# A twelve-layer perceiver in one kernel: an expert layer computed in turned form, and five more value units projected ahead of time

## What is computed

```
L2x:  q = xn @ Wq.T + bq;  k = ctx @ Wk.T + bk;  v = ctx @ Wv.T + bv      # 16 heads of 16
      out = softmax(q k.T / 4, masked) @ v;      x += out @ Wo.T + bo
L0a:  causal linear attention over the 128 rows, gated by a sigmoid;  x += ... @ W_proj
L0f:  y_e = (silu(xn @ W1_e.T) * (xn @ W2_e.T)) @ W3_e.T,  8 experts, 704 wide
      x += sum over the two best experts of score_e * y_e
L2f:  y_e = gelu(xn @ w_up_e.T) @ w_down_e.T,  8 experts, 1024 wide
      out = sum_e weight_e * y_e   (weight_e is zero but for the best two)
      x += layernorm(out) + xn
```

## Time and profile before

| | |
|---|---|
| median of 3 runs | 1596.67 us (1592.42 to 1596.86) |
| profiled execution | 1588.98 us |
| its span, first to last instruction | 1587.2 us |
| mean granted clock of TensorE | 0.992 |
| TensorE busy (matmul, weight load) | 1508.6 us, 1107.0 us |
| VectorE, ScalarE busy | 973.9 us, 954.2 us |

### The profile page before, as it was taken

One profiled execution on the slowest core, in us unless ns is written; L12 is line 12 of the kernel. 1 busy time (PEld: TensorE's weight loads), 2 busy tenths in 40 slices (PEclk: granted clock), 3 DMA queues, 4 the chain that ended last, 5 costly groups with the idle time before them and its releaser, 6 DMA issues.

```text
span 1587.2 us, 33990 instructions
## 1 busy us (share of the span) xinstructions
PE 1508.6 (95%) x13838; PEld 1107.0 (70%) x13838; DVE 973.9 (61%) x1860; ACT 954.2 (60%) x1453; POOL 9.7 (1%) x22
## 2 busy tenths in 40 slices
PE   6999999899999999999998999999999999998899
PEld 5766587667677767777776666777777777776664
DVE  5523323657777688776775325776767676767631
ACT  3121042238887888887883214887777777778711
POOL 0000000000000000000000000000000000000000
PEclk9999999799999999999999999999999999999999
DMA  9576855264535353444312466443434343323346
GB/s 392 235 282 262 303 195 213 83 234 178 177 113 173 134 201 119 152 152 149 114 45 114 174 236 227 146 168 119 153 117 153 115 154 117 141 94 109 131 180 270
DMA packets 56165, 270.81 MB, mean 171 GB/s; under 512 B 6608, under 2 KB 6864, under 8 KB 49360
## 3 DMA queue, kind: packets, MB, share of 16 engines
q1 hardware_dynamic: 56016, 268.70, 46.3%
HBM read 161.33 MB, written 4.59 MB: 105 GB/s over the span
## 4 chain that ended last, share of the span: by engine, by line
PE 80%; DVE 8%; issue 5%; ACT 5%; DMA 2%; POOL 0%; SPq 0%; DVEq 0%; ACTq 0%
PE T L852 14%; PE O L875 9%; PE S L838 8%; PE O L852 7%; PE T L810 6%; PE T L823 5%; PE S L680 5%; PE O L1005 3%; PE O L810 3%; PE S L1158 3%; PE O L1187 3%; PE T L675 2%; PE O L823 2%; ACT sc L1273 2%; DVE sc L1703 2%
## 5 line engine op out<-in xcount | busy, mean ns | idle before, releaser
L1703 DVE CUSTOM_DVE_ANT_0 sc<-S,mask_bias,small 128x896 f32<-128x896 f32 x336 | 377.6, 1149 | 46.8 <-PE S L838 46.8
L1273 ACT ACTIVATE sc<-sc,small 128x1792 f32<-128x1792 f32 x168 | 300.1, 1786 | 2.6 <-DVE small L1703 1.0
L1259 ACT ACTIVATE pT<-T 128x512 f32<-128x512 f32 x366 | 212.2, 597 | 87.2 <-PE T L852 87.2
L852 PE MATMUL T<-consts,sc 128*128 128x128 f32 x1546 | 232.7, 281 | 5.0 <-ACT sc L1273 3.1
L875 PEld LDWEIGHTS O<-pT,arena 128*32 128x32 f32 x6272 | 164.9, 110 | 74.8 <-issue 72.3
L852 PEld LDWEIGHTS T<-consts,sc 128*128 128x128 f32 x1546 | 168.9, 141 | 60.9 <-issue 39.7
L875 PE MATMUL O<-pT,arena 128*32 128x128 f32 x6272 | 194.4, 274 | 9.0 <-ACT pT L1259 9.0
L838 PE MATMUL S<-keys,q 64*128 64x512 f32 (+1 forms) x896 | 151.3, 415 | 10.1 <-DVE small L1703 9.9
L1669 DVE COPY pT<-T 128x512 f32<-128x512 f32 x150 | 103.6, 690 | 79.2 <-PE T L852 78.5
L1259 ACT ACTIVATE pT<-O 128x512 f32<-128x512 f32 x194 | 115.9, 597 | 52.4 <-PE O L852 52.4
L810 PE MATMUL T<-ctx_in,packs 128*128 128x448 f32 x320 | 133.4, 541 | 1.1 <-issue 1.1
(11 more groups left out here) (368 smaller groups left out, 1830.2 us busy)
## 6 DMA issues: line engine op xcount, KB each, us to landing
keys<-keys_hl SPq DMA_DIRECT2D x224, 448.0 KB, 4.5
ctx_in<-in_ctx_cols SPq DMA_DIRECT2D x46, 896.0 KB, 5.2
wide<-in_ctx_rows SPq DMA_DIRECT2D x14, 896.0 KB, 4.6
wide<-in_up_L0f SPq DMA_DIRECT2D x8, 1408.0 KB, 8.0
sc<-in_ctx_cols SPq DMA_DIRECT2D x10, 896.0 KB, 5.6
wide<-in_up_L2f SPq DMA_DIRECT2D x8, 1024.0 KB, 6.6
wide<-in_down_L2f SPq DMA_DIRECT2D x8, 1024.0 KB, 4.8
wide<-in_up_L3f SPq DMA_DIRECT2D x4, 2048.0 KB, 9.2
```

The costliest lines, as they stand in the source:

```text
L852: last = nc.tensor.transpose(ring(plan, u)[:, t * P:(t + 1) * P], weights_of(2 * m + i)[:, b * P:(b + 1) * P], ident)
L1259: nc.scalar.activation(pT2[:, g * BANK:(g + 1) * BANK], ring(plan, u), ACT.Copy).then_inc(s["t_act"], 1)
L1273: nc.scalar.activation(weights_of(n), weights_of(n), ACT.Exp, bias=n_best[c % 2][:, h:h + 1], scale=-1.0, accum_out=l_new[c % 2][:, h:h + ...
L1703: V.tensor_tensor_reduce(weights_of(n)[:, i * HC:(i + 1) * HC], S4f[:, n % 2 * 2 * BANK:n % 2 * 2 * BANK + HC], mask_bias[:, i * HC:(i + 1 ...
```

## The change

**L2f** gets its own form, `dense`. The up weights are the stationary operand, in blocks of 128 x 128, and xT with its 128 columns is the moving one. So the hidden values come out already turned, and there are no transposes. ScalarE's Gelu writes them from PSUM to one of two buffers in `arena`, where the down product reads them. The expert's weight is applied behind the down product, by VectorE, in one multiply-add into `yacc`. TensorE's order is up(0), up(1), down(0), up(2), down(1) and so on, written out without a loop. The three `dense` at the end of the diff are those of TensorE, ScalarE and VectorE. SyncE's loads stay as they are.

**Held values.** `WHOLE` is (4, 6): chunk 6 is kept whole too, so there are 22 held units and ten in `AFTER`. The five new ones read chunk 6 from `ctx_in`. They stand in L0a's second norm, before `heads_products` (two), in `tail`, and in the norm of L0f; in these places they take the place of `warm` products. The new units lie in `wide`, behind the two weight buffers, and in `o_sb`. The store of the held values moves in SyncE's order: it now stands in front of the loads of expert 2 of L0f (`dump_held`), in four transfers.

```
-WHOLE = 4
-KEPT = {"L2x": [0 if c == 1 else 7 if c == WHOLE else 2 for c in range(7)], "L3x": [0] * 7}
+WHOLE = (4, 6)
+KEPT = {"L2x": [0 if c == 1 else 7 if c in WHOLE else 2 for c in range(7)], "L3x": [0] * 7}
...
+            def dump_held():
+                s = L["L0x"]
+                sp.wait_ge(s["held_taken"], len(PASSING))
+                sp.wait_ge(s["after_taken"], len(AFTER))
+                at = 0
+                for piece in (held_a, held_b, held_c, o_sb[:, :].rearrange("p (u n) -> p u n", u=1)):
+                    n = min(piece.shape[1], len(HELD) - at)
+                    sp.dma_start(held_out[:, at:at + n], piece[:, 0:n]).then_inc(s["held_out"], 16)
+                    at += n
...
                     load_pack(layers[1])
-                    sp.wait_ge(s["held_taken"], len(PASSING))
-                    sp.wait_ge(s["after_taken"], len(AFTER))
-                    sp.dma_start(held_out[:, 0:IN_ARENA], held_a).then_inc(s["held_out"], 16)
-                    sp.dma_start(held_out[:, IN_ARENA:len(HELD)], held_b).then_inc(s["held_out"], 16)
...
                     if i == 0:
                         load_first(layer)
+                    if layer == "L0f":
+                        dump_held()
                     with sp.Fori(1, E // 2) as n:
...
+                elif layer == "L0f":
+                    after(9, S4[:, 2])
+                    warm(T2[:, 0], 4)
                 elif layer != layers[0]:
                     warm(T2[:, 0], 11)
...
                     after(1, S4[:, 3])
-                    warm(T2[:, 1], 5)
+                    after(2, S4[:, 1])
...
+                elif layer == "L0a":
+                    after(8, S4[:, 1])
                 else:
                     warm(S4[:, 0], wait)
...
-                        pe.wait_ge(L["L0x"]["after_taken"], len(AFTER))
-                        warm(O2[:, 1], 11)
+                        after(6, T2[:, 1], 4)
+                        after(7, O2[:, 1], 5)
+                        pe.wait_ge(L["L0x"]["after_taken"], 6)
                     need(pe, "dve", f"{layer}.qblk")
                     heads_products(layer, "A")
...
+            def dense(layer):
+
+                s = L[layer]
+                m = KD * FF[layer]
+
+                def up(e):
+                    b = e % 2
+                    w = fb[:, b, 0:m].rearrange("p (k n) -> p k n", k=KD)
+                    pe.wait_ge(s[f"up_in{b}"], 16 * (e // 2 + 1))
+                    for t in range(E):
+                        out = S4[:, 2 * b + t // 4, t % 4 * P:(t % 4 + 1) * P]
+                        last = product(out, w[:, :, t * P:(t + 1) * P], xT)
+                    last.then_inc(s["g_ready"], 1)
+                def down(e):
+                    b = e % 2
+                    w = fb[:, b, m:m + E * D].rearrange("p (t n) -> p t n", n=D)
+                    pe.wait_ge(s[f"down_in{b}"], 16 * (e // 2 + 1))
+                    pe.wait_ge(s["t_act"], e + 1)
+                    if e >= 2:
+                        pe.wait_ge(s["y_taken"], e - 1)
+                    product(O2[:, b, 0:D], hidden(b), w, E).then_inc(s["y_ready"], 1)
+                up(0)
+                for e in range(1, E):
+                    up(e)
+                    down(e - 1)
+                down(E - 1)
...
+            def dense(layer):
+
+                s = L[layer]
+                for e in range(E):
+                    b = e % 2
+                    act.wait_ge(s["g_ready"], e + 1)
+                    if e >= 2:
+                        act.wait_ge(s["y_ready"], e - 1)
+                    nc.scalar.activation(arena[:, b * 1024:(b + 1) * 1024].rearrange("p (i n) -> p i n", i=2),
+                                         S4[:, 2 * b:2 * b + 2], ACT.Gelu).then_inc(s["t_act"], 1)
...
+            def dense(layer):
+
+                s = L[layer]
+                for e in range(E):
+                    dve.wait_ge(s["y_ready"], e + 1)
+                    V.scalar_tensor_tensor(yacc, O2[:, e % 2, 0:D], wts[:, e:e + 1], yacc, ALU.mult, ALU.add) \
+                        .then_inc(s["y_taken"], 1)
+                    dve.wait_ge(s["y_taken"], e + 1)
```

More of the change, by code:

```diff
@@ L197 @@
 IN_ARENA = (NK - HELD_AT) // (2 * D)
-assert KD * D + (len(HELD) - IN_ARENA) * 2 * D <= CH
+IN_MASK = (CH - KD * D) // (2 * D)
+IN_WIDE = 4
+assert len(HELD) <= IN_ARENA + IN_MASK + IN_WIDE + 1
 PLANS = {layer: Plan(layer) for layer in VALUE_STEPS}
@@ L280, in build, with hidden @@
         gated = arena[:, 3200:4224]
+        def hidden(b):
+            return arena[:, b * 1024:(b + 1) * 1024].rearrange("p (t n) -> p t n", t=E)
         tokensT = work[:, 0:KD * E * SLOTS].rearrange("p (k n) -> p k n", k=KD)
@@ L395, in build @@
         held_a = arena[:, HELD_AT:HELD_AT + IN_ARENA * 2 * D].rearrange("p (u n) -> p u n", n=2 * D)
-        held_b = mask_bias[:, KD * D:KD * D + (len(HELD) - IN_ARENA) * 2 * D].rearrange("p (u n) -> p u n", n=2 * D)
+        held_b = mask_bias[:, KD * D:KD * D + IN_MASK * 2 * D].rearrange("p (u n) -> p u n", n=2 * D)
+        held_c = wide[:, 12288:12288 + IN_WIDE * 2 * D].rearrange("p (u n) -> p u n", n=2 * D)
         def held(of):
             n = HELD.index(of)
-            return held_a[:, n] if n < IN_ARENA else held_b[:, n - IN_ARENA]
+            if n < IN_ARENA:
+                return held_a[:, n]
+            if n < IN_ARENA + IN_MASK:
+                return held_b[:, n - IN_ARENA]
+            n -= IN_ARENA + IN_MASK
+            return held_c[:, n] if n < IN_WIDE else o_sb[:, :]
         held_out = nc.dram_tensor("held_values", (P, len(HELD) * 2 * D), F32, kind="Internal").ap()
@@ L543, in load_held @@
                         n, units = HELD.index((c, 0)), plan.kept[c]
-                        sp.wait_ge(L["L0x"]["held_out"], 32)
+                        sp.wait_ge(L["L0x"]["held_out"], 64)
                         if c >= 2:
@@ L708, in after @@
                     pe.wait_ge(s["after_taken"], free)
-                b = AFTER[n][1]
-                chunk = sc[:, 0:2, :].rearrange("p h (k n) -> p h k n", k=KD)
+                c, b = AFTER[n]
+                chunk = ctx_in if c == NC - 1 else sc[:, 0:2, :].rearrange("p h (k n) -> p h k n", k=KD)
                 for t in (2 * b, 2 * b + 1):
@@ L771, in qkv @@
                     pe.wait_ge(L["L3x"]["early_taken"], 1)
+                elif layer == "L0a":
+                    pe.wait_ge(L["L0x"]["after_taken"], 3)
                 product(S4[:, 0], src, w[:, :, 0:2 * D])
@@ L774, in qkv @@
                 if layer == "L0a":
-                    after(2, T2[:, 1])
-                    after(3, O2[:, 1])
-                    after(4, S4[:, 3], 2)
+                    after(3, T2[:, 1])
+                    after(4, O2[:, 1])
+                    after(5, S4[:, 3], 2)
                 if layer == "L1a":
@@ L1025, in expert @@
                         last.then_inc(s["t_ready"], 1)
+                if layer == "L0f":
+                    pe.wait_ge(L["L0x"]["after_taken"], len(AFTER))
                 expert(0, 0, 0, True)
@@ L1081, in _ @@
                         pe.wait_ge(L["L3x"]["early_taken"], 4)
+                    else:
+                        pe.wait_ge(L["L0x"]["after_taken"], 8)
                     for b in range(4):
@@ L1141, in _ @@
                     done("pe", product(O2[:, 0, 0:E], xT, pk(layer, "gate", KD)), f"{layer}.logit")
-                    (dispatched if layer == "L3f" else experts)(layer)
+                    (dispatched if layer == "L3f" else dense if layer == "L2f" else experts)(layer)
                 elif layer == "L1x":
@@ L1369, in take_early, with take_after @@
                                      ACT.Copy).then_inc(s["early_taken"], 1)
+            def take_after(n, bank):
+                act.wait_ge(L["L0x"]["after_ready"], n + 1)
+                nc.scalar.activation(held(AFTER[n]), bank, ACT.Copy).then_inc(L["L0x"]["after_taken"], 1)
             for layer in layers:
@@ L1382, in _ @@
                 elif layer == "L0a":
-                    def take_after(n, bank):
-                        act.wait_ge(L["L0x"]["after_ready"], n + 1)
-                        nc.scalar.activation(held(AFTER[n]), bank, ACT.Copy).then_inc(L["L0x"]["after_taken"], 1)
                     take_after(0, S4[:, 2])
                     take_after(1, S4[:, 3])
+                    take_after(2, S4[:, 1])
                     need(act, "dve", f"{layer}.g")
                     done("act", nc.scalar.activation(x2[:, :], x2[:, :], ACT.Sigmoid, accum_out=row), f"{layer}.sig")
-                    take_after(2, T2[:, 1])
-                    take_after(3, O2[:, 1])
-                    take_after(4, S4[:, 3])
+                    take_after(3, T2[:, 1])
+                    take_after(4, O2[:, 1])
+                    take_after(5, S4[:, 3])
+                    take_after(6, T2[:, 1])
+                    take_after(7, O2[:, 1])
+                    take_after(8, S4[:, 1])
+                    take_after(9, S4[:, 2])
```

(4 more changed lines are left out.)

## The result

The changed kernel takes 1587.54 us in the median of 14 runs (1583.06 to 1592.37), the kernel before 1593.86 us in the median of 14 runs beside them. The ratio is 0.9962 (95% interval 0.995 to 0.9975), which is 6.1 us less (4.0 to 8.0). The forecast was 7.6 us less.

The account below looks back on a forecast made before the run. TensorE, busy 95% of the span, was taken as the bound. Terms -8.3 - 7.5 + 0.7 + 5.1 + 2.4 = -7.6 us took 1588.98 to 1581.4, carried to the median as 1589.1 us; range 1580 to 1595.

Parts of the forecast that it names:

- L2x, -8.3 us: L2x, chunk 5: five value units fewer on TensorE, 75.24 us becoming like chunk 3's 66.95; 8.3 us gained.
- L2f's own work, -9.0 us: L2f on TensorE: transposes and two waits gone, up products at 3.58 us; 65.55 us becomes 56.5, 9.0 less.
- the rival with 0.22 a record: L2f's new up products: load and stream don't overlap, 0.22 us a record; +18.7 us in all, 1615; chance 0.06.
- L2f's weights, +1.5 us: L2f: up products start 0.5 us late for their weights at every second expert, three in the layer; +1.5 us.
- L0a, +0.7 us: L0a and L0f's norm: five more value units replace warm-up products and fill idle time; 0.5 to 1.0, taken as +0.7 us.
- L0f's wait, +5.1 us: L0f: expert 2's up weights queue behind the moved store, landing at 96.5 when TensorE wants them at 91.4; +5.1 us.
- The clock behind it, +2.4 us: L0f, after the wait: the clock falls to half speed for about 5 us; +2.4 us, from zero to 5.
- The other stages, nothing: Outside L2x, L2f, L0a and L0f: no term in the sum; after L0f's wait nothing is given back.
- Rival 1: L0f: the store does not delay TensorE, so 5.1 + 2.4 go; -15.1 us, 1581.6; chance 0.15.
- rival 2: L2f and L0f: transfers bind more, with later weights, slower store and longer low clock; -2.8 us, 1593.9; chance 0.15.

Follow-up runs that it names:

- warm_wait: The changed kernel with 54 warm-up records of 128 columns run while TensorE waits in L0f for expert 2's up weights; 1583.9 us, 0.9958 against before.

## Why the prediction was right, and where it was not

The direction, the range and the kind of mechanism held: a gain of 17.3 us in two stages, more than half of it taken back, mainly by a wait that did not exist before. Step by step:

- **L2x, -8.3 us: right.** 530.21 to 521.9 us in the table, and chunk 5 at 66.96.
- **L2f's own work, -9.0 us: right.** 72.04 to 63.07 once the waits are out of it. Load and stream overlap at 0.112 us a record, and the rival with 0.22 a record is out. The Trainium skill, page "TensorE: Matmul & The Clock Gate", section "Part 3: Packing small matmuls" (The mechanism), lists that loads overlap matmuls in flight only when the row group differs; the trace does not agree, for here they overlap with all rows in use. The same section also lets a load go ahead when it targets a background weight buffer; the trace agrees with that one, but does not show such a buffer.
- **L2f's weights, +1.5 us: the step is mis-sized.** Three starts are late, as forecast. But the sum of the waits is 1.5 to 3.1 us in six profiles (2.8 in the first), and in five of the six one or two transfers take 7.6 to 8.5 us where I took the 6.8 of one pair and bounded by 7.2. Against the 63.07 us without waits the layer is 2.3 to 3.9 us longer in five of them, some 0.8 more than the waits themselves, or 0.27 for each stop and start. In the first it is 5.2 us longer: behind its wait of 2.05 us came 1.7 us of low clock.
- **L0a, +0.7 us: right for the units alone** (30.00 against 29.48 in three profiles), but the low clock in the tail adds up to 3.7 us more in others. That it can happen was not in the sum.
- **L0f's wait, +5.1 us: 5.5 to 6.7 us in four profiles** (7.2 in warm_wait, warm-up products included). The order of service was right. The rate was not quite: about 380 KB a us from the store's first landing to the weights, where I took 400.
- **The clock behind it, +2.4 us: 1.6 to 3.05 us.**
- **The other stages, nothing: -0.9 us in L1a and -1.4 in L2a.** I had said that nothing is given back. L1a's goes with the wait in L0f and L2a's with the new held values in all eleven profiles; the cause is open.

With the terms as measured, L2f and L0f by their stages, the sum is -8.3 - 9.0 + 0.5 + (2.3 to 5.2) + (8.4 to 10.2) = -6.1 to -1.4 us, smaller than the forecast. With the 2.3 us of L1a and L2a it is -8.4 to -3.7, and the medians' -6.1 (4.0 to 8.0 less) lies in its middle. So that -7.6 came near is in part luck: the two costs of late weights were put too low, and two gains that I had not seen stood against them. Carrying the difference over to the median of the runs shown (1596.67) gave 1589.1; the median of 14 runs of the kernel before is 1593.86, 2.8 lower. Rival 1, that the store delays nothing, was wrong; rival 2 had the right direction for two sizes.

What stays open: why the clock falls in L0a's tail, in L1a, in L2a and in L3a in some profiles and not in others. Not tried.

## What to carry to other kernels

A step that is moved to another place in a queue's program costs what stands behind it: ask which load is due next, and add up the bytes ahead of it. Before the work is moved, see whether part of it is ready at the old place; here 17 of 22 units were, and splitting the store was worth 8 to 9 us, where the whole change gave 6. When an engine gets faster, look again at every load that was issued with just enough lead, and issue it when its buffer is free, not in the order in which the buffers are used.

## What the runs showed of the hardware

Half clock (1.2 GHz) came not only behind idle time. In L3a, in L0a's tail and in L2a of the kernel before it came during or right behind 32 matmul records of 16 or 17 columns each, with TensorE busy throughout. The changed kernel in L3a (first profile): the narrow products, the warm-up products behind them, and the window:

```profile
1512.45 4.49 PE L1177 MATMUL O<-arena,ctx_in 128*128 128x16 f32 x32
1516.77 5.67 PE L707 MATMUL S<-consts 128*128 128x128 f32 x26
...
1515.00:1520.00 5.00, 5.00 (x26) 5.00 (x26) 2.20 (x6) 0.00 (x0) 0.55 (x1) 0.52 0.98 413
```

The kernel before had 3.75 and 3.15 us at the same place. It falls in some executions of the same program and not in others (L3a takes 11.85 or 14.78 us), and a stage differs by up to 4 us for it. Two profiles of kernels that differ by less than that are compared stage by stage, and over several profiles.
